# A macaron transformer on one core: the score mask written by ScalarE, the engines' orders changed, and the weight loads moved

## The reference, cut to what matters

```
q, k, v = split(shift_tokens(x) @ Wqkv)              # 16 heads of 64
q = rotary(l2norm(q) * qs);  k = rotary(l2norm(k) * ksc)
sim  = q_window @ [k_previous_window, k_window].T * 8    # windows of 32 tokens
sim  = where(mask, -max, sim);  attn = softmax(sim)
x = (attn @ [v_previous_window, v_window]) @ Wo + x
x = (a * gelu(gate)) @ W2 + b2 + x      # a, gate = layernorm(shift_tokens(x)) @ W1 + b1
```

## Time and profile before

| | |
|---|---|
| median of 3 runs | 3613.35 us (3610.72 to 3627.78) |
| the profiled execution | 3621.26 us |
| its span, first to last instruction | 3619.1 us |
| PE / PE weight loads busy | 3322.5 (92%) / 2535.6 (70%) |
| DVE / ACT / POOL busy | 2800.4 (77%) / 2482.6 (69%) / 2720.1 (75%) |
| granted TensorE clock, mean | 0.969 |
| DMA | 272.66 MB, 28.2% of 16 engines |

### The profile page before, as it was taken

How to read it: one execution, slowest core, us unless ns; L and a number is a source line. 1 busy time by engine, 2 the same in 40 slices (tenths; PEclk the granted TensorE clock), 3 DMA queues, 4 the chain that set the end, 5 groups by cost and what they waited for, 6 DMA issues and landing times. The chain is left out here.

```text
span 3619.1 us, 152088 instructions
## 1 busy us (share of the span) xinstructions
PE 3322.5 (92%) x64040; PEld 2535.6 (70%) x64040; DVE 2800.4 (77%) x4983; ACT 2482.6 (69%) x3080; POOL 2720.1 (75%) x2152
## 2 busy tenths in 40 slices
PE   6899999999999999998677899999999999999996
PEld 4777777777777777776335777777777777777774
DVE  5778878788878878876447788778888878878883
ACT  4677777777767777775225677777777777777773
POOL 5888888788878878875007888888888888888881
PEclk8999999999999999999889999999999999999998
DMA  3333333333333333332002333333333333333320
GB/s 96 77 83 82 80 83 82 78 86 79 79 84 78 80 87 77 81 88 64 6 0 67 79 85 82 80 84 78 83 86 78 81 83 80 81 83 77 78 74 25
DMA packets 208997, 272.66 MB, mean 75 GB/s; under 512 B 55748, under 2 KB 103744, under 8 KB 208320
## 3 DMA queue, kind: packets, MB, share of 16 engines
q1 hardware_dynamic: 208320, 262.94, 28.2%
HBM read 60.35 MB, written 1.05 MB: 17 GB/s over the span
## 5 line engine op out<-in xcount | busy, mean ns | idle before, releaser
L1240 POOL TENSOR_TENSOR V<-RAWQK,TAB 128x512 f32<-128x512 f32 x768 | 953.2, 1275 | 443.5 <-PE PS L340 434.3
L388 PE MATMUL PS<-WH,XH 128*128 128x512 f32 x1152 | 518.4, 450 | 99.9 <-ACT VS L770 86.3
L770 ACT ACTIVATE VS<-PS 128x1024 f32<-128x1024 f32 x192 | 196.5, 1023 | 481.0 <-PE PS L390 357.2
L1282 POOL TENSOR_TENSOR V<-V,U 128x1024 f32<-128x1024 f32 x192 | 455.6, 2373 | 14.9
L390 PE MATMUL PS<-WL,XH 128*128 128x512 f32 x1152 | 465.5, 404 | 0.0
L389 PE MATMUL PS<-WH,XL 128*128 128x512 f32 x1152 | 464.5, 403 | 0.0
L1266 POOL TENSOR_TENSOR V<-V,U 128x1024 f32<-128x1024 f32 x192 | 457.5, 2383 | 0.0
L1275 POOL TENSOR_TENSOR V<-V,RN 128x1024 f32<-128x1024 f32 x192 | 372.2, 1938 | 93.7 <-DVE RN L918 92.1
L340 PEld LDWEIGHTS PS<-EYE,V 128*128 128x128 f32 x3072 | 348.2, 141 | 110.2 <-issue 99.0
L510 PEld LDWEIGHTS PS<-OT,WO 128*128 128x128 f32 x3072 | 373.6, 192 | 21.4 <-issue 5.1
L340 PE MATMUL PS<-EYE,V 128*128 128x128 f32 x3072 | 371.3, 274 | 10.3 <-ACT OT L777 5.1
(11 more groups left out here) (162 smaller groups left out, 7100.0 us busy)
## 6 DMA issues: line engine op xcount, KB each, us to landing
V<-VS SPq DMA_DIRECT2D x3072, 64.0 KB
ROTB<-c_rot SPq DMA_DIRECT2D x192, 128.0 KB, 2.5
WSTAGE<-wqkv SPq DMA_DIRECT2D x33, 512.0 KB
WO<-wo SPq DMA_DIRECT2D x12, 512.0 KB, 3.8
W<-w SPq DMA_DIRECT2D x12, 341.0 KB, 3.1
QKS<-qks SPq DMA_DIRECT2D x12, 128.0 KB, 3.7
W<-w SPq DMA_DIRECT2D x12, 114.0 KB
RAWQK<-x SPq DMA_DIRECT2D x4, 256.0 KB, 3.7
```

What stands on the lines that cost most here:

```text
L388: pe.matmul(o, XH[:, p, :], WH[:, w, cols], start=True, stop=False)
L1240: ins = pool.tensor_tensor(paired(V[:, k])[:, :, :, h * half:(h + 1) * half], split(RAWQK[:, k])[:, :, :, (1 - h) * half:(2 - h) * half], ...
L1282: pool.tensor_tensor(V[:, 1], V[:, 1], U[:, 1], ALU.add).then_inc(k_turned, 1)
```

## The change

The mask of each chunk is written into the two score banks by ScalarE (`seed_scores`), behind the copy of the transposed queries, and PE waits for it (`seeded`) in place of its two mask matmuls. So that the matmuls of the scores add to what ScalarE has written, the transposes set `start` only at the first tile of a bank. The maximum's subtraction writes PR in SBUF, and the exponential works in place there; what waited for the exponential to free the banks now waits for the subtraction. PE's loop has the scores of chunk t-1 at the end of slot t. The loops of ScalarE, DVE and POOL have new orders. In SP's queue, the three thirds of Wqkv are loaded at chunks 1, 8 and 12 of a layer, W1 at 9 and W2 at 11.

```
+WQKV_AT, W1_AT, W2_AT, ATTN_AT = (1, 8, 12), 9, 11, 11
@@ turn (all transposes)
-                                   is_transpose=True, start=True, stop=True, skip_group_check=True)
+                                   is_transpose=True, start=(h % 4 == 0), stop=True, skip_group_check=True)
@@ PE, queries / turn_queries / scores_a: use(exp_done, ...) becomes use(shifted, ...)
@@ PE, scores_a
-                    for r in range(2):
-                        pe.matmul(PS[:, B_S + r, :], EYEB[:, :], rep(MASK[:, 1 if c % CH == 0 else 0, :], [P, NP_, 2 * WIN], 1),
-                                  start=True, stop=False, skip_group_check=True)
+                    if live(c + SEED_LAG):
+                        pe.wait_ge(seeded, seed_count(inv, c))
...
@@ PE's loop
-                    scores_a(t - 2)
-                    scores_b(t - 2)
                     values(t - 1)
...
                     ffn_third(t - 2)
+                    scores_a(t - 1)
+                    scores_b(t - 1)
@@ ScalarE
+                def seed_scores(c):
+                    if not live(c) or not live(c + SEED_LAG):
+                        return
+                    act.wait_ge(q_kept, count(inv, c))
+                    act.activation(rows(B_S).rearrange("p r (j k) -> p r j k", k=2 * WIN),
+                                   MASKF[:, 1 if c % CH == 0 else 0, :].unsqueeze(1).unsqueeze(1).broadcast_to([P, 2, NP_, 2 * WIN]),
+                                   ACT.Copy).then_inc(seeded, 1)
...
-                    held(p_rows, count(inv, c - 1))
-                    held(sum_done, count(inv, c - 1))
-                    if inv == 0 and c == 0:
-                        act.wait_ge(w_split, 3)
-                    act.activation(PR[:, :, :].rearrange("p (j r) k -> p r j k", r=2),
-                                   rows(B_S).rearrange("p r (j k) -> p r j k", k=2 * WIN), ACT.Exp).then_inc(exp_done, 1)
+                    act.activation(PR[:, :, :], PR[:, :, :], ACT.Exp).then_inc(exp_done, 1)
@@ ScalarE's loop
+                    keep_weights(t - 3)
+                    keep_halo(t - 3)
                     copy_queries(t - 1)
...
                     keep_queries(t - 2)
+                    seed_scores(t - 2)
                     square_queries(t - 1)
+                    ffn_late(t - 3)
                     shift(t)
-                    ffn_late(t - 3)
                     keep_values(t - 1)
-                    keep_halo(t - 2)
                     exponentials(t - 2)
                     copy_keys(t)
-                    keep_weights(t - 2)
@@ DVE, row_max
-                    dve.tensor_tensor(s, s, rep(MX[:, :, :], [P, 2, NP_, 2 * WIN], 3), ALU.subtract).then_inc(shifted, 1)
+                    held(p_rows, count(inv, c - 1))
+                    if inv == 0 and c == 0:
+                        dve.wait_ge(w_split, 3)
+                    dve.tensor_tensor(PR[:, :, :].rearrange("p (j r) k -> p r j k", r=2), s,
+                                      rep(MX[:, :, :], [P, 2, NP_, 2 * WIN], 3), ALU.subtract).then_inc(shifted, 1)
@@ DVE's loop
+                    cos_queries(t - 1)
                     row_sum(t - 3)
...
                     norm(t - 1)
+                    cos_keys(t)
                     add_back(t - 4)
-                    cos_keys(t)
                     scale_keys(t - 1)
-                    cos_queries(t)
@@ POOL's loop
+                    add_keys(t - 2)
                     sin_queries(t - 2)
                     low_part(t - 1)
-                    add_keys(t - 2)
                     add_queries(t - 2)
@@ SP's loop
-                    if i in (1, 5, 9) and w + 1 < 2 * DEPTH:
-                        k = i // 4
+                    if i in WQKV_AT and w + 1 < 2 * DEPTH:
+                        k = WQKV_AT.index(i)
...
-                    if c >= CH and i == LAG:
+                    if c >= CH and i == W1_AT:
...
-                    if c >= CH and i == LAG + 2:
+                    if c >= CH and i == W2_AT:
```

More of the change, by code:

```diff
@@ L204, in build @@
         q_rows = sem("q_rows"); k_rows = sem("k_rows"); q_kept = sem("q_kept"); k_kept = sem("k_kept"); halo_kept = sem("halo_kept")
-        scored = [sem("scored%d" % r) for r in range(2)]; shifted = sem("shifted"); exp_done = sem("exp_done"); sum_done = sem("sum_done")
+        scored = [sem("scored%d" % r) for r in range(2)]; seeded = sem("seeded"); shifted = sem("shifted"); exp_done = sem("exp_done"); sum_done = sem("sum_done")
         p_rows = sem("p_rows"); p_kept = sem("p_kept"); v2_even = sem("v2_even"); v2_odd = sem("v2_odd")
@@ L240, in v2_count, with seed_count @@
             return ((inv * NCH + c) // 2 + 1) * V2_INC
+        def seed_count(inv, c):
+            return inv * (NCH - SEED_LAG) + c + 1
         def phase(n):
@@ L398, in queries @@
                     pe.wait_ge(xs_low, count(inv, c))
-                    after(use(exp_done, c - 2), use(exp_done, c - 2), use(q_kept, c - 2), use(uq_done, c - 1))
+                    after(use(shifted, c - 2), use(shifted, c - 2), use(q_kept, c - 2), use(uq_done, c - 1))
                     project(0, c, B_Q).then_inc(q_raw, 1)
@@ L423, in turn_queries @@
                     pe.wait_ge(q_scaled, count(inv, c))
-                    after(use(uq_done, c + 1), use(exp_done, c - 1), use(exp_done, c - 1), use(q_kept, c - 1))
+                    after(use(uq_done, c + 1), use(shifted, c - 1), use(shifted, c - 1), use(q_kept, c - 1))
                     turn(lambda h: V[:, 0, 2 * h:2 * h + 2, :].rearrange("p r d -> p (r d)"), B_TQ).then_inc(q_rows, 1)
@@ L447, in scores_a @@
                         return
-                    after(use(q_kept, c), use(uq_done, c + 1), use(exp_done, c - 1), use(exp_done, c - 1))
-                    for r in range(2):
-                        pe.matmul(PS[:, B_S + r, :], EYEB[:, :], rep(MASK[:, 1 if c % CH == 0 else 0, :], [P, NP_, 2 * WIN], 1),
-                                  start=True, stop=False, skip_group_check=True)
+                    after(use(q_kept, c), use(uq_done, c + 1), use(shifted, c - 1), use(shifted, c - 1))
+                    if live(c + SEED_LAG):
+                        pe.wait_ge(seeded, seed_count(inv, c))
+                    else:
+                        for r in range(2):
+                            pe.matmul(PS[:, B_S + r, :], EYEB[:, :],
+                                      rep(MASK[:, 1 if c % CH == 0 else 0, :], [P, NP_, 2 * WIN], 1),
+                                      start=True, stop=False, skip_group_check=True)
                     pe.wait_ge(q_kept, count(inv, c))
@@ L1388, in stack @@
                             "l p n -> p (l n)")).then_inc(w_in, 16)
-                    if i == 11 and w + 1 < 2 * DEPTH:
+                    if i == ATTN_AT and w + 1 < 2 * DEPTH:
                         held(projected, inv * NCH + c // CH * CH)
```

## The result

| | before | after |
|---|---|---|
| median of the compared runs, us | 3610.82 (3607.09 to 3627.78, 5 runs) | 3590.34 (3589.19 to 3594.78, 5 runs) |
| ratio, 95% interval | | 0.994 (0.9919 to 0.9962) |
| profiled execution, its span, us | 3621.26, 3619.1 | 3590.14, 3587.6 |
| mean granted clock | 0.969 | 0.972 |
| busy PE, DVE, ACT, POOL | 92%, 77%, 69%, 75% | 91%, 78%, 75%, 76% |

A gain of 0.6% where 2.6% was forecast (3520, range 3440 to 3580). Differences between kernels are therefore taken from their ratios, at 3.6 us for each 0.001; every ratio has an interval of about ±0.002 to 0.004, so ±7 to 15 us, and a difference of two ratios one of ±12 to 18. Sums over a trace are from one execution of each kernel.

What follows compares the result with a forecast made beforehand. PE was taken as the steady-state bound at 16.34 us a slot, with SP's waits for POOL's split adding stalls. 3621.3 - 112 + 24 - 10 + 5 = 3528, less 8 for the runs' median: 3520, range 3440 to 3580.

Steps and rivals of the forecast that it cites:

- Part 1: SP's queue: the new load chunks end SP's waits for POOL's split and PE's stalls behind them, -112 us.
- Rival 3: SP's stalls only move to the new chunks, as loads crowd the window copies' landing: 3632 us, chance 0.05.
- Part 3: POOL's addition ahead of the low part: no slot under 16.05 us, eating the mask's gain; +24 us net.
- Part 2: Mask moved from PE to ScalarE: 0.52 us a slot off PE, 100 us in all if nothing takes it back.
- the first layers: First layer of each stack: seed in the open, +0.48 us in some 12 slots, +5 us.
- rival 1: The mask's time taken off PE, the most used engine, survives: 3400 to 3436 us, chance 0.20 wholly or in part.
- The by-product: PE's short stops inside the scores (37.1 us in 41 places) are hidden where keys wait for POOL: -10 us.
- R: Follow-up theory: late signals ahead of short score matmuls make PE run dry; stops 60 to 75 us, time 3550 to 3570.

Runs made afterwards that it cites:

- run 1: Kernel before with only the new load chunks (1, 8, 12; W1 at 9, W2 at 11), mask on PE, old orders: 3510.47 us, ratio 0.9685.
- run 8: Kernel before with the new load chunks and POOL's addition of the keys moved ahead, mask on PE, all else old: 3546.9 us, ratio 0.9785.
- run 4: Changed kernel with the mask back on PE's two matmuls and no seed; new orders, loads and PR path kept: 3525.09 us, ratio 0.9726.
- run 7: Kernel before with new loads, seed by ScalarE, subtraction into PR and new start flags; ScalarE, DVE and POOL in old orders: 3567.45 us, ratio 0.9852.
- runs 3: Changed kernel with POOL's old order (addition of the keys behind the low part), all else as changed: 3565.61 us, ratio 0.9836.
- run 9: run 1 plus one PE wait ahead of its mask matmuls, for the squares of the next queries; no work added: 3566.94 us, ratio 0.984.
- run 11: run 7 with the seed only in 120 of 192 chunks, where it came early; PE's mask matmuls in the other 72: 3520.51 us, ratio 0.9727.
- run 5: Changed kernel plus two zero-weight matmuls per chunk, ahead of the scores and behind the wait for the seed: 3588.6 us, ratio 0.9903.
- run 6: Changed kernel plus the same two zero-weight matmuls per chunk, placed in the projection of the values: 3608.23 us, ratio 0.9967.

## Why the prediction was wrong

**What the changed kernel is made of**, by ratios: loads -114 (run 1), POOL's order +36 (run 8 over 1), the orders of ScalarE and DVE -21 (run 4 over 8), the seed +77 (the change over run 4). The sum is -22, the measured one -22; the last step closes it by construction, but run 7 over run 1 gives the seed +60 on its own.

**Part 1, the loads: right.** -112 was forecast, -114 measured, and SP's wait for POOL's split and the stalls of PE that hung on it are gone. Rival 3 falls with it.

**Part 3, POOL's loop: right.** PE's keys now wait for the low part in 90 places. The four slots were put at 65.9 and the window of them is 66.4. The +24 of the forecast was the four slots with the mask gone as well, so it isn't to be set beside run 8. With the mask on PE the same floor of 16.05 lifts only the slot from A to B (15.19), by 0.86 in each of 46 groups, some 40 us; run 8 measured +36. What ScalarE's and DVE's orders do was put at 0 and is worth -21 with the mask on PE (the subtraction into PR is part of that step), and nothing with the seed (runs 3 and 7, 0.9836 and 0.9852, the same within their intervals).

**Part 2, the seed: the step that failed.** The forecast took 0.52 us of mask off PE's slots, had the seed give it back in slot A alone, and called it hidden in B, C and D: "Natural slots of PE are then 15.35, 16.63, 15.57, 16.40", together 63.95 against 65.35, so -64 us in 46 groups for the seed by itself, and +5 in the first layers. Only POOL's loop was to take the rest. Measured, the seed by itself (run 7, without POOL's new order) costs 60 us, and 77 in the changed kernel. By the starts of the keys, as the forecast has them, the slots of run 7 are 16.08, 16.63, 16.49 and 16.87 in the median, 66.1 together: only B to C came as computed. That the four slots of the changed kernel came out near 65.9 is therefore in part luck.

The same slots from the first score matmul of a chunk to that of the next, on PE's timelines (medians over both stacks, first layers left out, us; one execution each):

```
                                        run 1   run 9   run 7   run 11  change
A to B                                  17.73   17.16   16.88   17.04   17.38
B to C                                  16.09   16.09   15.93   15.89   15.89
C to D                                  16.98   17.00   17.50   17.50   17.22
D to A                                  15.23   15.98   15.77   15.52   16.11
sum of the medians                      66.02   66.23   66.09   65.95   66.60
sum of the means                        66.48   67.59   67.71   66.78   67.90
slots over 1 us above their median         10      20      23      17      17
  what these are longer by, in all       14.8    46.3    58.3    25.3    46.2
  with a clock of 0.50 in a part of them    2       8      11       5      12
```

First, the regular pattern gains nothing, with POOL's loop or without: 66.09 in run 7, 65.95 in run 11 and 66.02 in run 1, which still has the mask on PE. So rival 1 (the mask's time survives) fails without POOL's loop too. The seed itself is in time in B to D, as forecast: its end leads the scores by 1.33, 0.46 and 0.46 us in the median. But it pushes ScalarE's later work back. From C to D, the slot of the gelus, the 0.52 of the mask is gone and the slot is still 0.52 longer (16.98 to 17.50, runs 7 and 11), together the seed's own 1.03; in run 9, which has the lateness without the work, it is 17.00. ScalarE had only 0.45 us to spare where it was looked at, and PE's wait for the exponentials grows. The forecast did count the seed among ScalarE's work ahead of the gelus, but only together with the shift's new place (16.35 for C to D); without that new place it let C to D fall to 15.57. The place was right and the cause too narrow. In slot A PE waits 0.7 us for the seed, in the median.

Second, single long slots, which the forecast didn't have. They make 43 of the 58 us between the executions of run 7 and run 1, and 32 of the 64 between those of run 9 and run 1. Run 1 has stops of 1.5 to 1.9 us in its scores too, and its long slots are mostly 1.1 to 1.5 longer. In the kernels with a late signal many are 3 to 5 us longer, with a stop of about 2 us and a granted clock of 0.50 behind it. The mean granted clock shows it over the whole span: 0.980 in run 1, 0.976 in run 9 and 0.975 in run 7. Estimated from 0.980 and 0.975, 38 us more at half clock in run 7 cost PE some 19. Why a late signal turns more of the stops into stretches at the lower clock is not shown.

Third, the first layers: 5 was forecast (0.48 in 12 slots, which is 5.8). PE waits there in 22 chunks, not 12, and mostly for 1.4 us, not 0.48; but the mask's time is a gain there. From the first scores of a stack to those of its second layer, the two stacks together are 6 us longer than in run 1 in run 7, 15 in run 9, which keeps the mask's work, and 18 in the changed kernel, whose POOL order counts there too (15 in run 8). The term was near for the seed alone.

**What lateness costs.** Run 9 over 1 gives 56 us, run 7 over 11 gives 45, each ±18. PE is idle directly ahead of the scores or their mask for 53.5 us in run 9 and 57.8 in run 7, against 7.7 in run 1: 40 slots A at 0.6 to 0.7, and 22 of the 32 chunks of the first layers. Against run 1 the profiled execution of run 9 is 64 us longer: 46 of them are these waits and, estimated from granted clocks of 0.980 and 0.976, some 16 are the lower clock. That accounts for run 9.

In run 7 against run 1, PE's time adds up so (spans, one execution each): mask matmuls -101, waits ahead of the scores +50, stops inside them +12, waits for the exponentials +15, all other idle time +21, and all other matmuls together +61, which is +58. The half clock explains about 19 of the 61; the rest is not traced to a cause. So the cost of lateness is accounted for, and the lost gain in the gelus' slot is seen, but where the other lost 0.52s go stays open.

**The by-product** of the forecast, "they are hidden: -10", is wrong in sign: the stops inside the scores rose from 37.1 us in 41 places to 44.8 in 45 (74.3 in 88 with the waits for the seed that stand under "issue"). In run 7 they are 50.1, in run 11 45.8, in run 9 38.8. That late signals directly ahead of short matmuls make them was R's idea, and runs 5 and 6 (46.5 and 46.4) don't bear it out. What they come from stays open.

**The busiest engine.** The Trainium skill (Perfetto Trace Analysis, Identifying the Most-Contended Engine) has the most-contended engine optimised first, as rival 1 says, but it doesn't take TensorE by its matmul busy share: there it goes by the weight loads' share and the matmul rate. PE's weight loads are busy for 70% of the span before, below DVE's 77% and POOL's 75%, so the page doesn't single PE out as rival 1 did with its 92%. The traces agree that this 92% promised too much: taking 100 us from PE made the kernel 60 us slower (run 7 over 1), and putting 100 us back among the values cost 10 us, no more than its interval (run 6 over the change).

**The best version measured** is run 1, the loads alone: 3510.47, ratio 0.9685 to the kernel before and, through it, 0.9685 / 0.994 = 0.974 to the changed one.

## What to carry to other kernels

Moving work off the fullest engine moves a signal too: ask when the helper's signal comes against the one that the full engine waited for already, and charge the difference in every slot where that was the last one (here some 1 us later, 62 waits in 192 chunks, 45 to 56 us in all). Then look at the helper's own shortest slack in the period (0.45 us here against 1.03 of new work), since a mean share of 69% busy says nothing of it. Look also at the slots that are longer than the rest, since an undisturbed stretch (66.4 here, close to the forecast's 65.9) hides them. When a row of waits goes under "issue", check the helper's timeline before calling it a stop. Measure the parts apart: the one plain part of this change, the times of the loads, was worth more than the whole.

## What was unexpected of the hardware

- ScalarE wrote the mask into two PSUM banks in 1.03 us per 128x1024 (192 times), the same as its copies out of PSUM (1.02 to 1.04).
- A semaphore that PE gets about 1 us later, with no work added, cost 56 us (±18) in 192 chunks, of which PE waited in 62 (run 9).
- Some stops of about 2 us in a run of 128 short matmuls are followed by the lower clock: granted clock 0.58 in the 4.10 us behind one of 2.10 us, the projection's matmuls at 0.63 us a piece against 0.40, and 1.00 in the undisturbed stretch before it. In the loads-only kernel eight of the ten longest slots kept 1.00.
- Two extra matmuls of 128x512 in bfloat16 per chunk were 23 us (±12) cheaper ahead of the scores (run 5) than among the values (run 6), where the granted clock was lower in every execution (0.971 to 0.976 against 0.978 to 0.980).
